# A two-layer transformer block on one core: one maximum instruction over two adjacent PSUM banks in layer 1

## The reference, cut to what matters

```python
Q = x @ W_Q.T; K = x @ W_K.T; V = x @ W_V.T       # 2 batches x 1024 tokens x 128
Q, K, V -> 16 heads of 8 values each
attn = einsum('bhqd,bhkd->bhqk', Q, K) / sqrt(8)
attn = where(causal, attn, -inf)
probs = softmax(attn, axis=-1)
y = einsum('bhqk,bhkd->bhqd', probs, V)
return y @ W_O.T
```

## Time and profile before

| | |
|---|---|
| median of 3 runs | 1192.28 us |
| the profiled execution | 1190.6 us, its span 1188.8 us |
| TensorE matmul busy | 1063.3 us (89%) |
| VectorE busy | 811.4 us (68%) |
| ScalarE busy | 646.5 us (54%) |
| GpSimd busy | 210.0 us (18%) |
| maximum instructions, L1605, both layers | 896, 511.9 us |
| chain that ended last: TensorE, VectorE, ScalarE | 69%, 19%, 6% |
| layer 1's attention | about 639 to 900 us |

### The profile page before, as it was taken

One profiled execution on the slowest core, in us unless ns is written; L12 is line 12 of the kernel. 1 busy time (PEld: TensorE's weight loads), 2 busy tenths in 40 slices (PEclk: granted clock), 3 DMA queues, 4 the chain that ended last, 5 costly groups with the idle time before them and its releaser, 6 DMA issues.

```text
span 1188.8 us, 19388 instructions
## 1 busy us (share of the span) xinstructions
PE 1063.3 (89%) x7308; PEld 490.5 (41%) x7308; DVE 811.4 (68%) x1625; ACT 646.5 (54%) x1259; POOL 210.0 (18%) x327
## 2 busy tenths in 40 slices
PE   5699999999999999999977888899889999888767
PEld 4455555552222222222234333334334468543444
DVE  7656666667887888875377778888674156655654
ACT  4522222226898888889733366677565432442534
POOL 2244554510010101010003011113221000001100
PEclk9899999999999999999976799899898999999888
DMA  4684112001010111000023422211322020000431
GB/s 128 201 229 140 50 66 81 2 1 28 25 43 30 43 30 34 12 20 20 11 66 97 151 66 75 60 45 42 126 86 88 10 80 1 1 1 0 143 143 36
DMA packets 57398, 74.63 MB, mean 63 GB/s; under 512 B 15720, under 2 KB 35032, under 8 KB 55512
## 3 DMA queue, kind: packets, MB, share of 16 engines
q1 hardware_dynamic: 48516, 62.13, 16.5%
q10 hardware_dynamic: 8788, 11.26, 3.4%
HBM read 58.18 MB, written 14.54 MB: 61 GB/s over the span
## 4 chain that ended last, share of the span: by engine, by line
PE 69%; DVE 19%; ACT 6%; issue 3%; DMA 2%; SPq 1%; ACTq 0%; POOL 0%; DVEq 0%
PE PS L1835 67%; DVE mx L1605 9%; ACT arena L1090 4%; DMA sums<-arena 1%; PE PS L1848 1%; DVE arena L1809 1%; DVE arena L1404 1%; DVE arena L1379 1%; DVE arena L1364 0%; DVE arena L1407 0%; DVE small L1795 0%; SPq L689 0%; DMA arena<-in_L_attn_x 0%; PE PS L2307 0%; DVE fw L1700 0%
## 5 line engine op out<-in xcount | busy, mean ns | idle before, releaser
L1835 PE MATMUL PS<-arena 128*32 128x512 f32 (+10 forms) x3656 | 568.1, 479 | 50.3 <-DVE mx L1605 22.8
L1605 DVE TENSOR_REDUCE mx<-PS 128x1 f32<-128x512 f32 (+3 forms) x896 | 511.9, 625 | 88.7 <-PE PS L1835 86.8
L1090 ACT ACTIVATE arena<-PS 128x512 f32<-128x512 f32 (+3 forms) x896 | 435.3, 558 | 149.3 <-PE PS L1835 145.0
L1835 PEld LDWEIGHTS PS<-arena 128*32 128x32 f32 (+3 forms) x3656 | 149.1, 104 | 409.5 <-ACT arena L1090 183.6
L1835 PE MATMUL PS<-x_hi,w_hi_lo 128*128 128x512 f32 x320 | 145.7, 496 | 6.8 <-ACT fw L1133 2.3
L1133 ACT ACTIVATE fw<-PS 128x512 f32<-128x512 f32 x80 | 47.8, 598 | 168.0 <-PE PS L1835 168.0
L1700 DVE TENSOR_TENSOR fw<-PS,fw 128x512 f32<-128x512 f32 x80 | 55.3, 692 | 79.2 <-PE PS L1835 76.6
L1835 PE MATMUL PS<-fw 128*128 128x512 f32 (+3 forms) x184 | 98.4, 620 | 0.0
L1001 POOL TENSOR_TENSOR fw<-fw,arena 128x512 f32<-128x512 f32 x64 | 81.8, 1280 | 76.1 <-DVE fw L1700 76.1
L925 POOL TENSOR_TENSOR arena<-arena,fw 128x512 f32<-128x512 f32 x31 | 39.4, 1272 | 262.8 <-DMA fw<-sum_dram 262.8
L1835 PEld LDWEIGHTS PS<-x_hi,w_hi_lo 128*128 128x128 f32 x320 | 61.5, 192 | 37.8 <-issue 21.2
(11 more groups left out here) (317 smaller groups left out, 1110.1 us busy)
## 6 DMA issues: line engine op xcount, KB each, us to landing
arena<-comb_dram SPq DMA_DIRECT2D x14, 1024.0 KB, 4.8
arena<-comb_dram SPq DMA_DIRECT2D x18, 512.0 KB, 7.4
fw<-sum_dram SPq DMA_DIRECT2D x31, 256.0 KB
q_dram<-arena SPq DMA_DIRECT2D x24, 256.0 KB, 3.7
k_dram<-arena SPq DMA_DIRECT2D x24, 256.0 KB, 4.0
arena<-k_dram ACTq DMA_DIRECT2D x20, 204.0 KB
arena<-q_dram ACTq DMA_DIRECT2D x20, 192.0 KB
arena<-drev_dram SPq DMA_DIRECT2D x16, 192.0 KB, 6.9
```

Of the source, the lines that this page charges most:

```text
L1090: s.activation(Pr[:, m % 8, 0:w], st_bank(l, m, 0, w), ACT.Exp).then_inc(A["e_done"], 1)
L1605: v.reduce_max(mx[:, H % 2, kh, n:n + 1], bank(ring_bank[l][U], 0, w), axis=AX.X, negate=True).then_inc(A["ring_free"], 1)
L1835: return nc.tensor.matmul(out_, lhsT, rhs, start=start, stop=stop)
```

## The change

In layer 1 two S units of adjacent ring banks (heads j = 1 and 0, or 3 and 2) are reduced by one VectorE instruction with an output of two values for each partition. It waits for both units and raises `ring_free` by 2. The ring of four banks becomes two pairs of banks. M and C take a pair of places each. K moves from one to two S units into the next half's, M from five to six. The maxima of the odd heads now lie in front of those of the even ones, and `max_rows` reads them so. Layer 0 stays as it is.

```diff
-COMBINE_AFTER, MAX_AFTER = 1, (8, 5)
+COMBINE_AFTER, MAX_AFTER = (1, 2), (8, 6)
@@ s_stream
-        late += [("K", H, COMBINE_AFTER), ("M", H, MAX_AFTER[layer])]
+        late += [("K", H, COMBINE_AFTER[layer]), ("M", H, MAX_AFTER[layer])]
@@ ring_of
-            n += 1
+            n += 2 if layer == 1 and what[0] != "S" else 1
@@ max_rows (SyncE)
-                sp.wait_ge(A["ring_free"], place[l]["M", H] + 1)
+                sp.wait_ge(A["ring_free"], place[l]["M", H] + (2 if l else 1))
-                    row, first = 64 * (j % 2) + ROWS, 12 * (PAIRS * (j % 2) + j // 2)
+                    row, first = 64 * (j % 2) + ROWS, 12 * (PAIRS * ((j + l) % 2) + j // 2)
@@ sequence (VectorE)
-                        dve.wait_ge(A["ring_full"], U + 1)
+                        if l == 1 and what[0] == "S":
+                            _, H, j, q, kh, w = what
+                            if j % 2 == 1:
+                                assert U % 2 == 0
+                                dve.wait_ge(A["ring_full"], U + 2)
+                                n = 4 * (j // 2) + q % 4
+                                first = 512 * ring_bank[l][U]
+                                two = PS[:, first:first + 1024].rearrange("p (a w) -> p a w", a=2)[:, :, 0:w]
+                                out = mx[:, H % 2, kh, :].rearrange("p (a n) -> p a n", a=2)[:, :, n]
+                                v.reduce_max(out, two, axis=AX.X, negate=True).then_inc(A["ring_free"], 2)
+                            continue
+                        dve.wait_ge(A["ring_full"], U + (2 if l else 1))
@@ M and C: their matmul and their copy
-                            ... .then_inc(A["ring_free"], 1)
+                            ... .then_inc(A["ring_free"], 2 if l else 1)
-                        ... .then_inc(A["ring_full"], 1)
+                        ... .then_inc(A["ring_full"], 2 if l else 1)
```

More of the change, by code:

```diff
@@ L821, in comb_out @@
             def comb_out():
-                sp.wait_ge(att[1]["ring_free"], place[1]["C",] + 1)
+                sp.wait_ge(att[1]["ring_free"], place[1]["C",] + 2)
                 sp.dma_start(comb_dram[1], combT[:, :]).then_inc(comb_stored, 16)
@@ L1609, in sequence @@
                                 dve.wait_ge(A["m_ld"], 64 * (H - 1))
-                            v.tensor_copy(mrow[:, H % 2, :], bank(ring_bank[l][U], 0, P)[0:48, :]).then_inc(A["ring_free"], 1)
+                            v.tensor_copy(mrow[:, H % 2, :], bank(ring_bank[l][U], 0, P)[0:48, :]).then_inc(A["ring_free"], 2 if l else 1)
                         else:
-                            v.tensor_copy(combT[:, :], bank(ring_bank[l][U], 0, P)).then_inc(A["ring_free"], 1)
+                            v.tensor_copy(combT[:, :], bank(ring_bank[l][U], 0, P)).then_inc(A["ring_free"], 2 if l else 1)
                 def invert(H):
@@ L1972, in ring_unit @@
                     if what[0] == "M":
-                        mm(bank(ring_bank[l][U], 0, P)[0:48, :], mparts[:, what[1] % 2, :], identb[:, :]).then_inc(A["ring_full"], 1)
+                        mm(bank(ring_bank[l][U], 0, P)[0:48, :], mparts[:, what[1] % 2, :], identb[:, :]).then_inc(A["ring_full"], 2 if l else 1)
                     else:
                         nc.tensor.transpose(bank(ring_bank[l][U], 0, P), gate_bufs(1)[4][:, :, :].rearrange("p e t -> p (e t)"),
-                                            ident[:, :]).then_inc(A["ring_full"], 1)
+                                            ident[:, :]).then_inc(A["ring_full"], 2 if l else 1)
                 def st_adds(H, i, j, dst):
```

## The result

The changed kernel takes 1240.87 us, the median of 4 runs (1236.11 to 1242.99), against 1192.49 us for the kernel before. The ratio is 1.0397, with a 95% interval of 1.0355 to 1.044: slower by 48 us. The forecast was 1218 us in a range to 1243. The direction and the mechanism came out; the size is nearly twice what was summed. The profiled execution has a span of 1234.3 us, 45.5 over that of before.

The account below looks back on a forecast made before the run. Quiet steps were taken as tight on TensorE, with VectorE and ScalarE close behind. 1190.6 + 27.5 of stalls - 2 of gain gave 1216 us, written as 1218 because the profiled execution lay 1.7 us under the median; range 1201 to 1243.

Parts of the forecast that it names:

- The loop: Layer 1 attention, once a step: unit, value product, last unit, pair's reduce, in series; 3.12 us in i2 against 2.53.
- The rival in which VectorE decides: Where reduces run without a gap, saved VectorE time comes back and no stall appears: 1183 us; chance 0.10.
- The rival in which the stall is hidden: Stalls fall into the 82.9 us of waits for exponentials, only E0 and E1 lengthen: 1197 us; chance 0.08.
- The lead and half 0: First 64 units, 32 pairs: VectorE runs without a gap, so joining gains; 2 us taken with other gapless stretches.
- E2 and E3: Steps E2 and E3: the loop gives 2.2 us each, nothing added; i0's wait takes up what E3 loses.
- i3, i6 and i7: Step i3: loop 2.6 us, nothing added; i6 2.90 us against 2.13; i7 2.78 us against 2.21.
- The six steps that were written off: i2 twice, i6, i7 twice and E0, already longer than the loop: 3.9 us taken off 31.4.
- i0 and i1 of halves 3 to 13: Steps i0 and i1: loop 2.5 and 2.4 us, nothing added, being bound by ScalarE and TensorE already.
- The clock: Rival: stalls drop a quarter of some 80 steps to the lower clock, 24 us more, 1242 us; chance 0.14.
- The saving: Layer 1's joined reduces: VectorE loses 192 x 0.14 = 27 us of busy time.
- The price of M between two pairs of E1: E0 to E1: M takes a pair of banks, so E1's second pair waits for its first; 3.60 us against 2.77, +0.83.
- The rival of late M rows: M's DMAs set the start of a half; one unit more delay costs 1 us at 13 starts: 1231 us; chance 0.08.

Follow-up runs that it names:

- h2: The changed kernel with single reduces for the 64 units of the lead and half 0, pairs from half 1 on: 1233.53 us.
- h1: The changed kernel's plan with pairs only for units of 128 and 256 columns, single reduces for wider ones: 1205.5 us.
- w1: The changed kernel with two back-to-back reduces per pair, which wait for both units and free both banks at the end: 1244.67 us.
- m1: The changed kernel with M after ten units of the next half instead of six in layer 1: 1264.77 us.
- w2: The changed kernel's plan with the single reduces of before, each freeing its own bank: 1200.4 us, 1.0041 of the kernel before.

## Why the prediction was right, and where its size was off

**The loop: right.** Ten steps agree with the sums to 0.10 us, and taking the value product out of it returns most of the loss. The rival in which VectorE decides fell with the slower time; its price of 1183 us did not follow from its own terms either, for half of 24.9 us and the 2 us of the lead give 1178 us. The rival in which the stall is hidden fell for the quiet steps, where the wait turned up in full, but not for the half starts, as told below. (The 0.24 and 0.47 us that are given against the first rival as TensorE's idle time are VectorE's; the argument needs it so.)

**The sum: 27.5 - 2 us forecast, 45.5 measured in the profiled executions.** The other 20 us are the balance of several terms, by the trace:
- *The lead and half 0*, forecast as 2 us of gain, cost 7.6 us (691.26 against 683.63 us at half 1's second step). This is the term that failed worst, 9.6 us. It was priced by VectorE having no gap there; but with 8 to 10 units a step and the value product between units of a pair, at the lower clock, the same loop closes several times a step, as I read it. That the pairs make it is shown by h2, which is 6.5 us earlier there; about 1 us stays, and so is not the pairs'.
- *E2 and E3*, set to nothing. The loop gave 2.2 us for each; they measured 2.13 and 2.14 against 1.98 and 1.61, and the following i0 did not take it up: 2.76 us after as 2.80 before. Six times 0.68, 4 us; h1 shows the same lengths.
- *i3, i6 and i7* were 0.05 to 0.1 us over the sum, 0.25 us an odd half, seven times: 2 us.
- *The six steps that were written off*, 3.9 us, because they were longer than the loop already. They grew by 3.4 us all the same (i2 of half 5 by 0.14, i2 of half 11 by 0.70, i6 and i7 of half 5 by 0.16 and 0.64, i7 of half 13 by 0.74, E0 of half 4 by 1.05).
- *i0 and i1 of halves 3 to 13*, set to nothing, took 9 us less in all. Half 11's i0 fell from 7.60 to 3.60 us and half 13's from 4.90 to 2.77. Before, VectorE waited there for the DMA of the softmax sums, 4.7 us in half 11, and TensorE waited 4.5 us for VectorE behind it; with more time between, that wait is nearly gone (the waits for those sums in all, before and after, stand below). So the hidden stall was real at the half starts. How much of it is one execution's chance is open: in w1, with the same loops, half 11's i0 took 6.00 us. Three steps i1 (halves 3, 7 and 13) ran at clock 1.00 in 2.39 or 2.40 us, where before they took 3.48 to 3.51 us at 0.54 to 0.61.
- *The clock.* Half a rival came true. The mean granted clock from 640 us to the end of the units is 0.83 (640 to 943 us), against 0.89 before (640 to 898 us). In half 0, 660 to 690 us is at 0.56, against 0.77 before. In the quiet odd halves the stalls of 0.6 us did not lower it: they are in nearly every step, and the clock keeps 1.00. Behind E0 it fell. There M adds two stalls to the one of the loop, and four of the six steps E1 behind it took 4.34 to 4.50 us and one 3.64, instead of 3.16. In half 10 TensorE stood still for 0.56, 0.61 and 0.67 us between 865.1 and 869.4 us, and for no longer at a time; the clock was 1.00 until then and 0.62 in E1. In half 12 it was the same, with 0.56, 0.61 and 0.56 us and then 0.61. In half 8 much the same stalls left it at 1.00. Before, the six steps E1 ran in 2.36 to 2.38 us. In m1, where M is not in E1, that of half 10 ran at 1.00. This is 5 us of E1 alone; no run here sets the clock by itself, so its share is read and not tested.

These terms come to about 15 us. The other 5 are, for the most part, E2 and E3 of halves 6 and 10 (2.6 us over the quiet ones) and 2 us behind the units; they were not taken apart.

```profile
DVE rsums L1620 <- DMA sums<-arena: 7.6, 3, 4.7
...
DVE rsums L1631 <- DMA sums<-arena: 0.6, 1, 0.6
```

```profile
660.00:690.00 30.00, 24.04 (x184) 10.41 (x183) 18.57 (x24) 10.55 (x23) 2.02 (x9) 0.56 0.29 90
...
832.00:835.80 3.80, 2.60 (x38) 1.49 (x36) 3.07 (x5) 2.79 (x6) 2.64 (x7) 1.00 0.24 86
835.80:839.00 3.20, 2.49 (x35) 1.08 (x32) 1.54 (x2) 1.53 (x4) 1.90 (x4) 1.00 0.04 8
...
855.00:860.00 5.00, 4.18 (x51) 1.99 (x48) 3.28 (x5) 2.95 (x8) 1.39 (x3) 1.00 0.06 6
...
866.00:870.00 4.00, 2.69 (x40) 1.54 (x41) 2.97 (x5) 2.61 (x6) 3.03 (x7) 1.00 0.00 2
870.00:873.40 3.40, 2.97 (x32) 1.47 (x24) 1.56 (x2) 1.48 (x4) 1.50 (x4) 0.62 0.02 4
```

These windows (columns as in the earlier trace rows) are of the changed kernel: half 0, then E0 and E1 of half 8, a quiet i4 and i5, then E0 and E1 of half 10. The rule of the Trainium skill, page "TensorE: Matmul & The Clock Gate", section "A second HAM failure mode: psum-queue depth-cycling", is that small idle pieces between groups of products make the clock swing. The quiet step does not bear it out: there TensorE stalls in every step and the clock stays at its upper level of 2.4 GHz. E0 and E1 of half 10 agree with it: the clock fell from 1.00 with no single stall over 0.7 us ahead of it.

**The saving: wrong.** 27 us of VectorE's busy time were forecast; on the page it falls from 811.4 to 801.5 us, 10 us. The rows of before held it: 704 reduces of 682 ns are 480 us, but their busy time is 444.5 us, 631 ns each, because neighbours overlap. The price of an instruction in a run of them is its busy time over its count, not its mean duration. By the same rule, two of 512 against one are 1.26 against 1.20 us (115.6 us over 96), a saving of 0.06.

**M: right in size, only in part by the pairs.** The price of M between two pairs of E1 was forecast at +0.83 us and is +0.92, but +0.42 of it stand in w2 already, with single reduces. The rival of late M rows did not come in the changed kernel; m1 shows that it is real, for its four units more, one step, bring the waits of 14.0 us.

## What to carry to other kernels

Before joining two instructions that read a ring of buffers, draw the loop from a buffer's release back to its next filling, and put into it everything that the filling engine issues between the two parts of the pair: here a 1 us product, and behind it the doubled reduce, 3.1 us where a step needed 2.5. What counts is when the buffer comes back, not how many instructions give it back. And an overlap that the profile shows (count times mean well above busy time) means that most of the overhead to be saved has been saved already: here joining two saved 0.06 us and not 0.14.

## What the runs showed that was not expected

Moving the value product behind the fourth slot, a control for another question, beats both kernels: 1185.88 us, 0.9922 (0.9897 to 0.9946) of the kernel before, with single reduces and the old plan. In its 680 to 710 us the clock is 1.00, against 0.90 for the kernel before in the same window; i0 and i1 of its first pair of halves follow each other at 2.44 and 2.46 us. Which wait it shortens at the half starts was not tested.

A reduce over parts of two PSUM banks with an unread gap between them costs no more than one over adjacent columns: 942 ns for two of 384 against 957 ns for 768 adjacent ones, and 690 ns for two of 256 against 692 ns for 512.
